# Transposed scores one pipeline step later, and the stack of row maxima as three one-partition transfers

## The reference, cut to what is computed

```python
x = x + layernorm(attention(layernorm(x), wq, wk, wv, wo))
x = x + layernorm(ffn(layernorm(x), W_base, b_base, W_gate, A, B))

# attention: rotary q and k, causal
scores = einsum('bqhd,bkhd->bhqk', q, k) / sqrt(16) + mask
attn = softmax(scores)
out = einsum('bhqk,bkhd->bqhd', attn, v).reshape(b, s, 512) @ wo

# ffn: top 2 of 8 experts, low rank, added to a dense layer
result = x @ W_base.T + b_base
delta = einsum('bner,eor->bno', h * route_w[..., None], B)
return result + delta
```

## Time and profile before

| | us |
|---|---|
| median of three runs (lowest, highest) | 267.73 (266.85, 270.82) |
| span of the profiled execution | 265.6 |
| PE busy | 212.1 (80%) |
| DVE busy | 170.5 (64%) |
| ACT busy | 135.9 (51%) |
| POOL busy | 117.9 (44%) |
| DMA: queue of SP, share of 16 engines | 43.8% |

### The profile page before, as it was taken

One profiled execution on the slowest core, in us unless ns is written; L12 is line 12 of the kernel. 1 busy time (PEld: TensorE's weight loads), 2 busy tenths in 40 slices (PEclk: granted clock), 3 DMA queues, 4 the chain that ended last, 5 costly groups with the idle time before them and its releaser, 6 DMA issues.

```text
span 265.6 us, 3792 instructions
## 1 busy us (share of the span) xinstructions
PE 212.1 (80%) x1304; PEld 130.1 (49%) x1304; DVE 170.5 (64%) x414; ACT 135.9 (51%) x238; POOL 117.9 (44%) x93
## 2 busy tenths in 40 slices
PE   0699999977757999699595999695497988997860
PEld 0575734433433444244343444143477967886750
DVE  1983437759738768547473771426457988889674
ACT  2241603312235878558545574643157485777771
POOL 8000506613095867748466334941551452332031
PEclk9999999999979999979998899999979999998985
DMA  6994069898930638666473222223321001110013
GB/s 185 367 379 158 12 233 210 260 299 160 263 114 4 151 115 285 147 161 109 151 147 128 72 88 84 88 76 132 135 68 39 2 0 41 39 42 4 36 41 118
DMA packets 34058, 34.14 MB, mean 129 GB/s; under 512 B 2808, under 2 KB 28536, under 8 KB 34040
## 3 DMA queue, kind: packets, MB, share of 16 engines
q1 hardware_dynamic: 34040, 33.91, 43.8%
HBM read 19.42 MB, written 14.29 MB: 127 GB/s over the span
## 4 chain that ended last, share of the span: by engine, by line
PE 30%; DMA 28%; DVE 22%; ACT 7%; issue 5%; SPq 5%; POOL 2%; POOLq 0%; DVEq 0%; ACTq 0%
DMA region_b<-mrow 10%; DMA den_pk<-o_scr 6%; PE ps L1086 4%; PE ps L1149 4%; DVE stats L743 4%; PE ps L1001 3%; DMA o_scr<-o_sb 3%; PE ps L1060 3%; PE ps L1101 3%; PE ps L977 3%; PE ps L991 3%; DMA region_b<-q_scr 2%; SPq L325 2%; DMA rden_bc<-r_scr 2%; DMA x_sb<-x 2%
## 5 line engine op out<-in xcount | busy, mean ns | idle before, releaser
L917 DVE TENSOR_REDUCE nmax<-ps 128x4 f32<-128x1024 f32 x32 | 39.1, 1223 | 25.3 <-PE ps L1060 25.3
L512 POOL TENSOR_SCALAR_AFFINE_SELECT region_a<-region_a 128x1024 f32<-128x1024 f32 x32 | 35.2, 1106 | 26.7 <-ACT region_a L689 26.6
L1086 PE MATMUL ps<-region_b,kst 99*128 99x512 bf16 x96 | 28.7, 405 | 14.5 <-DMA region_b<-mrow 13.4
L689 ACT ACTIVATE region_a<-ps 128x1024 f32<-128x1024 f32 x32 | 32.7, 1020 | 1.2 <-PE ps L1086 1.2
L686 ACT ACTIVATE region_a<-ps 128x512 f32<-128x512 f32 x32 | 19.1, 598 | 26.0 <-PE ps L1086 25.6
L991 PE MATMUL ps<-region_a,region_c 128*128 128x512 f32 x64 | 29.0, 598 | 0.0
L914 DVE TENSOR_REDUCE nmax<-ps 128x4 f32<-128x512 f32 x32 | 21.8, 683 | 8.4 <-PE ps L1044 8.4
L554 ACT ACTIVATE std<-mv,eps_sb 128x1 f32<-128x1 f32 x32 | 9.3, 293 | 32.3 <-DVE mv L744 32.3
L1101 PE MATMUL ps<-region_a,v_aug 128*32 128x512 f32 x192 | 25.2, 603 | 0.0
L548 ACT ACT_TABLE_LOAD x17 | 21.8, 1283 | 1.1 <-PEq L1246 0.8
L1060 PEld LDWEIGHTS ps<-kst,region_b 96*128 96x128 bf16 x256 | 18.3, 102 | 7.0 <-issue 1.7
(11 more groups left out here) (107 smaller groups left out, 436.6 us busy)
## 6 DMA issues: line engine op xcount, KB each, us to landing
region_b<-q_scr SPq DMA_DIRECT2D x8, 768.0 KB, 8.0
o_scr<-o_sb SPq DMA_DIRECT2D x8, 512.0 KB, 3.1
q_scr<-region_c SPq DMA_DIRECT2D x8, 384.0 KB, 3.6
x_sb<-x SPq DMA_DIRECT2D x8, 256.0 KB, 5.9
q_scr<-region_c SPq DMA_DIRECT2D x8, 256.0 KB, 3.5
attn_t<-o_scr SPq DMA_DIRECT2D x8, 256.0 KB
rden_bc<-r_scr SPq DMA_DIRECT2D x8, 256.0 KB
out<-region_b SPq DMA_DIRECT2D x8, 256.0 KB, 2.0
```

The lines of the kernel that those rows point to most:

```text
L512: pool.affine_select(out=blocks, in_=blocks, compare_op=ALU.is_ge, fill=0.0, base=0, pattern=[[0, 2], [0, REP], [1, P]], channel_multiplie ...
L689: nc.scalar.activation(probs[:, u % PRING, 1:3, :], ps[:, 4:6, :], ACT.Exp, scale=float(HEAD_DIM) ** -0.5).then_inc(exp_done, 1)
L917: nc.vector.tensor_reduce(nmax[:, gi % 2, 1, heads], ps[:, 1:3, :].rearrange("p a (r k) -> p r a k", r=REP), AX.XY, ALU.max, negate=True). ...
L1086: last = nc.tensor.matmul(ps[:, 3 + j, :], kst[0:TROWS, slot, k, kt * P:(kt + 1) * P], qst[0:TROWS, slot, k * REP:(k + 1) * REP, qt * P:(q ...
```

## The change

`ST_LAG` goes from 7 to 8: PE's `scores_t`, ACT's exponentials and POOL's mask come one step later against `scores`, while `turn_max`, `mrow` and `stack_max` stay at step 5 + 4g. `PV_LAG` goes from 12 to 13, so all that hangs on it (attend, the output copies, the four output transfers, `invert`, `divide`) moves by one step too, and `STEPS` grows from 43 to 44. The loads of `qst` and `kst` move from step 4g + 11 to 4g + 12. `stack_max` becomes three DMAs of 8 KB, each from 16 partitions of `mrow` to one partition of `qst`; the counts that ACT and PE wait for are three times as large.

```diff
-ST_LAG = 7
+ST_LAG = 8
 MAX_LAG = 5
-PV_LAG = 12
+PV_LAG = 13
 STEPS = 4 * (GROUPS - 1) + PV_LAG + 3
@@
             def stack_max(gi):
                 sp.wait_ge(mrow_ready, gi + 1)
-                sp.dma_start(qst[SROWS:TROWS, gi % RING, :, :], mrow[0:PARTS * GROUP_HEADS, gi % 2, :])\
-                    .then_inc(mrow_stacked[gi % 2], 16)
+                for part in range(PARTS):
+                    sp.dma_start(qst[SROWS + part:SROWS + part + 1, gi % RING, :, :],
+                                 mrow[part * GROUP_HEADS:(part + 1) * GROUP_HEADS, gi % 2, :])\
+                        .then_inc(mrow_stacked[gi % 2], 16)
@@
-                        act.wait_ge(mrow_stacked[gi % 2], 16 * (gi // 2))
+                        act.wait_ge(mrow_stacked[gi % 2], 16 * PARTS * (gi // 2))
@@
-                    pe.wait_ge(mrow_stacked[gi % 2], 16 * (gi // 2 + 1))
+                    pe.wait_ge(mrow_stacked[gi % 2], 16 * PARTS * (gi // 2 + 1))
```

## The result

The changed kernel takes 282.5 us (median of four runs, 281.4 to 283.1); the kernel before, run beside it, 269.3 (four runs, 266.9 to 272.5). The ratio is 1.060, interval 1.052 to 1.069: slower, where I had forecast 263.1 us. Ratios here come from undisturbed runs only, so they can differ from the quotient of two medians, which is 1.049 here.

The account below looks back on a forecast made before the run. PE's waits for the stack and SP's queue loop were taken to bind together. Gains of 1.1 us at the start, 3.5 net mid-attention, 0 in the tail: span 265.6 to 261.0, plus 2.1 for the median, 263.1 us; range 257.0 to 270.0.

Parts of the forecast that it names:

- What bounds the kernel: Attention: PE's transposed scores wait 13.4 us for the stack of maxima, and SP's queue loop binds at once.
- why the stack is late: SP's queue, groups 3 to 5: the stack stands right behind the 256 KB fetch, taking 6.9 and 6.7 us.
- One step more of cover: PE between turn_max and transposed scores: about 3.1 us more work, cover 7.8 us against 7.6 and 7.4 needed.
- by PE alone: Looking only at PE, the stack waits of groups 3 to 5 would be all but gone, with perhaps 3 us of slow clock.
- the 9.15 us: PE's summed waits for the stack in groups 3 to 5, expected to all but vanish.
- All of it has moved by the same step and its order is unchanged: Tail from 158 to 197 us: the latency chain keeps its order, starting and ending 4.6 us earlier.
- Order of SP's queue and the loop: SP's queue: stack ahead of the fetch but held behind spread and loads, extra issues 1.1 us, loop 15.1 us as before.
- The split into three: The stack's transfer over more engines: saves 0.4 us of landing (bounds 0 to 0.5), lost again to the last issue.
- Units 20 to 24 and the end: Late attention and tail: unit 24 at 151.2 instead of 155.79, a gain of 4.6 us carried to the end.
- The clock after a wait: PE after a stack wait: granted clock at 1.2 GHz, three matmuls taking 1.46 us instead of 0.82.
- Case 4: SP's queue: den_pk lands 14.4 us after the spread, loop 17.9 us, slower at 269.5 us; chance 0.16.
- case 3: Groups 3 to 5 wait as long as before, now for the load of q: a wash, 266 us; chance 0.15.

Follow-up runs that it names:

- experiment 7: Kernel before with fetch_out one step later, behind the stack in SP's queue; 268.4 us, ratio 0.996.
- experiment 10: Kernel before with fetch_out one step later, behind the stack, and the split's two casts as reductions; 267.9 us, ratio 0.989.
- experiment 14: Kernel before with the late fetch_out and the casts as reductions, run again in more rounds; 267.5 us, ratio 1.000.
- experiment 9: Changed kernel with the causal mask on one head of four and the split's casts as reductions; 269.0 us, ratio 1.011.
- experiment 1: Changed kernel with the stack as one transfer again, lags kept at 8 and 13; 280.9 us, ratio 1.032.
- experiment 2: Changed kernel with PV_LAG back at 12, ST_LAG 8 and three transfers kept; 272.7 us, ratio 1.012.
- experiment 12: Changed kernel with PV_LAG back at 12 and the split's two casts as reductions; 275.7 us, ratio 1.025.
- experiment 13: Kernel before with PV_LAG 13 alone (ST_LAG 7, one transfer); 289.8 us, ratio 1.077.
- experiment 6: Changed kernel with attend ahead of turn_max in PE's step; 281.0 us, ratio 1.038.
- experiment 3: Changed kernel with the causal mask on one head of four, so POOL's masks are shorter; 270.7 us, ratio 1.007.
- experiment 8: Changed kernel with the split's two casts written as reductions; 275.5 us, ratio 1.020.
- experiment 5: Kernel before with the stack as three transfers, lags 7 and 12 kept; 271.0 us, ratio 1.004.
- experiment 11: Kernel before with only the split's two casts as reductions; 271.3 us, ratio 1.014.

## Why the prediction was wrong, step by step

**What bounds the kernel: right; why the stack is late, in part.** The wait for the stack was there. That its place behind the fetch causes it is clear for group 3 only, whose 2.93 us are gone in experiments 7, 10 and 14. Ahead of the fetch the stack still costs 10.1 and 9.3 us in experiments 10 and 14. Two readings were off. The load of q does not drain 8.8 us after the spread: it lands 10.0 us after its issue at 114.83, 11.1 after the spread. And a DMA share of 0.29 is a mean over 16 engines and doesn't say that few of them were busy. That an issue behind spread and loads is held is in the rows; that a full queue holds it, no run shows.

**One step more of cover: right for the stack, wrong as a gain.** I wrote that "by PE alone" the 9.15 us would be all but gone. They are: PE's matmuls have no wait for the stack left behind that of group 0 (1.16 us, at 75.42), not even the 1 to 3 us that I gave groups 4 and 5. The failed step is in the words "by PE alone", and in "All of it has moved by the same step and its order is unchanged". `PV_LAG` hangs attend on another of four steps, while the split and `turn_max` stay where they are, and I put the wait behind the split at nothing. I listed DVE's split in the text ahead and never compared DVE's step with PE's. The rows for it were there: 0.68 + 1.22 for the reductions, 0.8 for the split, 1.8 us for PE's step without attend, that is 0.9 us a group as an estimate; measured without a hold, 0.62 and 0.74. Over groups 2 to 6 that is 3 to 4.5 us, a third to a half of the 9.15. The collision makes it 13.7 us there (0.7 before), and takes 1.8 more in group 1. Of this the forecast had no hint but one: the casts' mean of 351 ns against 181 for the same size.

**Order of SP's queue and the loop: right in form.** The three issues behind spread and loads took 3.14 and 5.20 us (4.78 and 5.43 in experiment 9; I had said 4 to 5.5 for the first and 1.1 more, so the first of after is short). The rows of after:

```profile
126.28 0.54 SPq L386 DMA_DIRECT2D rden_bc<-r_scr  x1
...
131.12 3.14 SPq L354 DMA_DIRECT2D region_b<-mrow  x3
...
142.56 0.52 SPq L386 DMA_DIRECT2D rden_bc<-r_scr  x1
...
145.57 5.20 SPq L354 DMA_DIRECT2D region_b<-mrow  x3
```

The spreads (the next at 157.46) are 16.3 and 14.9 us apart, in experiment 9 16.0 and 14.3 (from 117.84), for a forecast of 15.1. DVE waits 8.6 us for `den_pk`, 2 more than before (I said 2 to 5). But this loop starts at 126.28, not at 112.6: it was not what bound here.

**The split into three: right as far as measured.** Counted as 0.4 and lost again; on the kernel before 1.004 (0.998 to 1.009). In the changed kernel experiment 1 leaves it open.

**Units 20 to 24 and the end: wrong in time, right in form.** Unit 24 starts at 170.45, 14.7 us later than before, not 4.6 earlier. From there the tail repeats: the late store goes out at 184.88, 15.6 us behind before's 169.24, and the span is 15.6 longer.

**The clock after a wait: not as a rule.** I wrote that after a wait for the stack the clock is at its lower level. The rows show that it need not be: at 129.09, after 2.95 us, three matmuls take 0.82 us, and the granted clock is 1.00 from 129 to 133.

**The rivals.** None was on VectorE. Case 4, slower by the queue's loop, had the sign and not the mechanism. The wait for q that case 3 names did appear, once the trouble on DVE was taken away (8.5 and 12.0 us in experiments 2 and 12). With it the idea did not pay even without the trouble on DVE.

**What is shown and what isn't.** Shown: `PV_LAG` brings the wait and takes it away (2 and 13), and the cover by attend is a part of that (6); POOL's instruction length and the form of the casts set the stretch (3, 8); the three transfers don't cause these waits (1), and cost nothing on the kernel before (5). The sum of attention closes by the waits: of 15 us 5.9 are clock and 9.1 idle, and the idle time is the 14.2 that `turn_max` took, less the 10.9 that the stack gave back, and 5.8 of small waits. Not shown: why POOL's pieces fall on the split in groups 2, 3, 4 and 6 and in the one at 143 us not, and how much the three transfers cost in the changed kernel.

## What to carry to other kernels

When a lag moves in a pipeline with a period of four steps, write down for each engine what stands in each of the four, before and after, and compare the engines step by step: a step that loses its heavy PE work exposes whatever small VectorE work was hidden in it. Wherever VectorE casts or has two SBUF inputs on a short critical path, look what GpSimd does at that moment; a cast as a reduction over an axis of one element was not held in any of the kernels that had it here, though on the kernel before it gained nothing (experiment 11). And a wait removed is worth only the distance to the next one: here DVE's split, the load of q and `den_pk` stood close behind the stack, and each came forward when the one ahead of it was taken away.

## What the runs showed of the hardware

A VectorE cast or subtraction of 128 x 32, 0.18 us by itself, mostly takes about 1.0 us (up to 1.5) when it meets a GpSimd instruction of 1.1, and ends when that one ends; one cast took 3.15 us beside three masks in a row (experiment 7). Casts with means of 530 and 702 ns became 178 and 186 as reductions. After the stop of 3.16 us at 96.53 the granted clock is 0.50 until about 102 us (0.85 as a mean over attention, 0.94 before), so that eight matmuls of 1.07 us take 1.94; after stops of 2.95 us (129.09 in the kernel before) and 3.12 us (161.93 in the kernel after) it was still 1.00 for the first microsecond at least. Three small issues behind a 256 KB spread and the loads take 3.1 to 5.4 us, and 1.8 with an open queue.
